# Five edits in a two-layer decoder kernel: units of a scan among its first prelude, a quantisation loop as a pipeline, a delta rule's copies, four-head attention by portions, ternary weights beside the last norm

## The reference

```python
# 1 selective scan: causal 4-tap convolution, low-rank delta, then over time, 16 states per channel
h = dA * h + dBu;  y = einsum('bdn,bn->bd', h, c)
# 2 smooth-quantised expert, for each of the 4 batches: w1 (512 x 512), w2 (512 x 256)
s = maximum(sqrt(maximum(amax_x, EPS) / maximum(amax_w, EPS)), EPS)
xs = x / s;  ws = w * s
x_q = clip(round(xs / x_scale), -127, 127);  w_q = clip(round(ws / w_scale), -127, 127)
out = x_q @ w_q.T * x_scale * w_scale.T          # twice, with silu(gate) * up between
# 3 a mixture of 8 experts and a shared one
# 4 delta rule, 16 heads of 128, 512 steps of time
S = S * exp(g);  vd = (v - S @ k) * beta;  S = S + outer(k, vd);  o = S @ q
o = o * rsqrt(mean(o * o) + EPS) * o_norm_w * sigmoid(gate);  out = o @ Wo
# 5 cross attention, 32 heads of 16, with rotary positions
w = softmax(q k^T / 4);  attn = w @ v
# 6 ternary feed-forward, hidden width 1408
wq = clip(round(w / mean(|w|)), -1, 1);  xq = round(x * 127 / max|x|)
h = silu(bitlinear(x, w1)) * bitlinear(x, w2);  bitlinear(h, w3)
```

## Time and profile before

| what | us |
| --- | --- |
| median of three runs (6689.74 to 6696.33) | 6691.91 |
| profiled run | 6693.45 |
| its span | 6691.8 |
| PE busy | 5326.8 (80%) |
| PEld busy | 3517.8 (53%) |
| DVE busy | 4030.0 (60%) |
| ACT busy | 2628.2 (39%) |
| POOL busy | 2044.4 (31%) |

### The profile page before, as it was taken

One profiled execution on the slowest core, in us unless ns is written; L12 is line 12 of the kernel. 1 busy time (PEld: TensorE's weight loads), 2 busy tenths in 40 slices (PEclk: granted clock), 3 DMA queues, 4 the chain that ended last, 5 costly groups with the idle time before them and its releaser, 6 DMA issues. The chain is left out here.

```text
span 6691.8 us, 83945 instructions
## 1 busy us (share of the span) xinstructions
PE 5326.8 (80%) x24965; PEld 3517.8 (53%) x24965; DVE 4030.0 (60%) x6738; ACT 2628.2 (39%) x4831; POOL 2044.4 (31%) x2589
## 2 busy tenths in 40 slices
PE   4889437999478888888888888888887669999946
PEld 2666324555245556555565555655555335555513
DVE  4777663222277666666666666666666246666566
ACT  4555211111144444444444444444443116666512
POOL 2556100201244434344343443434434050000100
PEclk8999758999689999999999999999998789999978
DMA  2011004344311111111111111111110021111010
GB/s 55 27 26 26 19 19 180 117 135 149 109 48 46 31 48 41 37 46 37 48 41 37 46 37 48 41 37 36 37 48 19 23 85 49 43 43 43 30 52 25
DMA packets 349792, 344.90 MB, mean 52 GB/s; under 512 B 99552, under 2 KB 252640, under 8 KB 348160
## 3 DMA queue, kind: packets, MB, share of 16 engines
q1 hardware_dynamic: 335472, 286.73, 14.6%
q0 software_dynamic: 13984, 54.01, 2.3%
HBM read 264.76 MB, written 75.89 MB: 51 GB/s over the span
## 5 line engine op out<-in xcount | busy, mean ns | idle before, releaser
L1706 POOL TENSOR_TENSOR delta_rule_suffix<-delta_rule_suffix,delta_rule_prefix 128x256 f32<-128x256 f32 x448 | 498.9, 1114 | 1268.7 <-ACT delta_rule_prefix L1800 743.5
L2520 PE MATMUL attend_out_ps<-attend_probsT,attend_v_head 128*128 128x512 f32 x1024 | 481.5, 593 | 0.0
L2070 PE MATMUL delta_rule_level<-delta_rule_qk_second,delta_rule_k_first 128*128 128x128 f32 x3072 | 427.8, 283 | 51.8 <-DVE delta_rule_L_small L1879 40.3
L2046 PE MATMUL delta_rule_proj<-delta_rule_hT,delta_rule_w_qkv 128*128 128x512 f32 x1024 | 466.5, 599 | 0.0
L1697 POOL TENSOR_TENSOR delta_rule_k_first<-delta_rule_qk,delta_rule_suffix 128x256 f32<-128x256 f32 x384 | 303.3, 790 | 512.6 <-PE delta_rule_level L2058 485.5
L2070 PEld LDWEIGHTS delta_rule_level<-delta_rule_qk_second,delta_rule_k_first 128*128 128x128 f32 x3072 | 385.8, 195 | 103.2 <-issue 81.8
L2547 DVE TENSOR_REDUCE attend_top<-attend_scores 128x1 f32<-128x512 f32 x512 | 328.5, 683 | 158.3 <-PE attend_scores L2502 158.3
L1947 DVE TENSOR_TENSOR delta_rule_prefix<-delta_rule_prefix 128x256 f32<-128x256 f32 x448 | 287.5, 642 | 226.0 <-PE delta_rule_level L2058 187.3
L472 DVE TENSOR_TENSOR_SCAN scan_hs<-scan_decay,scan_inp 128x512 f32<-128x512 f32 x256 | 307.9, 1216 | 189.2 <-PE scan_inp L534 91.0
L309 POOL TENSOR_TENSOR scan_hc<-scan_hs,scan_c_rows 128x512 f32<-128x512 f32 x256 | 333.1, 1308 | 272.2 <-DVE scan_hs L472 253.4
L1890 DVE TENSOR_TENSOR delta_rule_qk_second<-delta_rule_qk,delta_rule_prefix 128x512 f32<-128x512 f32 x448 | 337.9, 754 | 45.9 <-issue 10.3
(11 more groups left out here) (463 smaller groups left out, 12036.1 us busy)
## 6 DMA issues: line engine op xcount, KB each, us to landing
moe_w_d<-in_w_down SPq DMA_DIRECT2D x39, 512.0 KB, 4.4
scan_c_rows<-bc_dram SPq DMA_DIRECT2D x64, 256.0 KB, 3.8
delta_rule_w_qkv<-in_kda_wq SPq DMA_DIRECT2D x64, 256.0 KB
delta_rule_w_qkv<-in_kda_wk SPq DMA_DIRECT2D x64, 256.0 KB
delta_rule_w_qkv<-in_kda_wv SPq DMA_DIRECT2D x64, 256.0 KB
delta_rule_inv_beta<-beta_dram SPq DMA_DIRECT2D x64, 256.0 KB
delta_rule_w_o<-in_kda_wo SPq DMA_DIRECT2D x64, 256.0 KB, 5.0
small_dram<-delta_rule_L_small SPq DMA_DIRECT2D x64, 256.0 KB, 2.0
```

What stands on the lines that cost most here:

```text
L1706: pool.tensor_tensor(first, first, whole_second, ALU.mult).then_inc(suffix_done, 1)
L2046: last = pe.matmul(to, w_qkv[p][:, i, k, :], hT[:, b % 2, k, :], start=(k == 0), stop=(k == DT - 1))
L2070: last = pe.matmul(level_ps[(i + 1) % 2][:, c, :], left, qk_second[:, i % 2, :, c * CHUNK // 2:(c + 1) * CHUNK // 2], start=True, stop=True)
L2520: last = pe.matmul(out_ps[:], v_head[:, j, i, :], probsT[:, j % 2, i, :], start=(j == 0 and i == 0), stop=(j == H - 1 and i == TPB - 1))
```

## The change

Five parts, one for each of five blocks.

**Scan.** Unit 0 goes at slot 36 of the first prelude, and 28 units of batch 0 share its remaining slots. The other 36 units of batch 0 take the 64 chores of batch 1 between them. The diagonals of batch 0 are made in slots 24 to 39.

```diff
+        FIRST_UNIT_AT = 36
             for j in range(UNITS):
                 chores(0, j)
-            for b in range(B):
+                if j >= FIRST_UNIT_AT:
+                    unit(0, j - FIRST_UNIT_AT)
+            for i in range(FIRST_UNIT_AT):
+                unit(0, UNITS - FIRST_UNIT_AT + i)
+                for j in range(i * UNITS // FIRST_UNIT_AT, (i + 1) * UNITS // FIRST_UNIT_AT):
+                    chores(1, j)
+            for b in range(1, B):
```

```diff
+    JOBS = [(b, lin) for lin in range(2) for b in range(B)]
+            def pipeline(*stages):
+                for at in range(N + len(stages) - 1):
+                    for slot in range(SLOTS):
+                        for d in reversed(range(len(stages))):
+                            if 0 <= at - d < N:
+                                stages[d](slot, at - d)
...
+                    def quantize(slot, i):
+                        if second:
+                            act.wait_ge(inv_ready, m + 1)
+                            reach(act, quantized, m - 1)
+                            for r in range(HALF_ROWS):
+                                last = act.activation(rounded[:, m % 2, r, 0:width], rows_ps[m % 2][r][:, 0:width], ACT.Identity,
+                                                      bias=round_up[:, 0:1], scale=row_inv[:, m % 2, r:r + 1])
+                            last.then_inc(rounded_done, 1)
+                            if q > 0:
+                                copy_turned(i, q - 1)
```

```diff
-        SQUARE_SLOT, NORM_SLOT, LN_SLOT, EXP_SLOT, GATED_SLOT, OUT_SLOT, ADD_SLOT = 12, 13, 14, 14, 17, 23, 25
+        SQUARE_SLOT, NORM_SLOT, LN_SLOT, EXP_SLOT, GATED_SLOT, OUT_SLOT, ADD_SLOT = 12, 13, 20, 20, 26, 23, 26
+        VD_COPY_SLOTS = (1, 4, 6, 10)
-                    if slot < 3 * CHUNKS and slot % 3 == 1:
-                        c = slot // 3
+                    if slot in VD_COPY_SLOTS:
+                        c = VD_COPY_SLOTS.index(slot)
                 def tail(slot, n):
+                    project(slot, n)
                     back(slot, n)
-                    project(slot, n)
-                            pe.wait_ge(o_inv_done, n + 1)
+                            pe.wait_ge(o_ln, n + 1)
```

```diff
+    GROUP = 4
+    WEIGH_AT = 1
+    COLS = 2 * X_DIM
-                    last = pe.matmul(out_ps[:], v_head[:, j, i, :], probsT[:, j % 2, i, :],
-                                     start=(j == 0 and i == 0), stop=(j == H - 1 and i == TPB - 1))
+                    for q in range(GROUP):
+                        j = half * GROUP + q
+                        last = pe.matmul(out_ps[q * COLS:(q + 1) * COLS, :], v_head[:, j, i, :], probsT[:, j, i, :],
+                                         start=(half == 0 and i == 0), stop=(half == 1 and i == TPB - 1))
...
                         turn(n, j, i)
-                        if i % 2 == 1 and not first:
-                            weigh(*before, i - 1)
-                            weigh(*before, i)
+                        if i == WEIGH_AT:
+                            if j >= GROUP:
+                                weigh(n, 0, j - GROUP)
+                            elif not first_tile:
+                                weigh(n - 1, 1, j)
```

```diff
+                        act.activation(flat_weights(i), w[:, i, :], ACT.Abs, accum_out=part[:, i:i + 1]).then_inc(part_done, 1)
+                        if i > 0:
+                            act.wait_ge(inv_ready, i)
+                            act.activation(w[:, i - 1, :], w[:, i - 1, :], ACT.Identity, bias=round_up[:, 0:1],
+                                           scale=inv[:, i - 1:i]).then_inc(rounded_up, 1)
...
+                        dve.tensor_scalar(w[:, i, :], w[:, i, :], ROUND, -1.0, ALU.subtract, ALU.max)
+                        dve.tensor_scalar(flat_weights(i), w[:, i, :], 1.0, None, ALU.min)
...
                         for c, (lo, n) in enumerate(FFN_CHUNKS):
+                            if c == 1 and not first:
+                                turn_act(t - 1)
```

More of the change, by code:

```diff
@@ new lines, in _, with scales, output @@
+                    for j in range(2):
+                        sp.wait_ge(w_loaded[j], 16 * N // 2)
+                @block.gpsimd
+                def _(pool):
+                    pool.memset(round_up[:], ROUND).then_inc(round_made, 1)
+                    def scales(slot, i):
+                        pass
+                    def output(slot, i):
+                        if slot == 0:
+                            along = row_scale[:, i % 2, JOBS[i][1], :]
+                            pool.wait_ge(inv_ready, PARTS_OF_JOB * (i + 1))
+                            reach(pool, acc_done, acc_item(i - 2, 0) + 1 if i >= 2 else 0)
+                            for r in range(TPB):
+                                last = pool.tensor_scalar(spread[:, i % 2, r, :], g["ones"][:], along[:, r:r + 1], None, ALU.mult)
+                            last.then_inc(spread_done, 1)
+                    pipeline(scales, scales, output)
@@ L708, in _ @@
-                            if lin == 0:
-                                dve.drain()
-                                dve.wait_ge(silu_done, b + 1)
-                                dve.tensor_tensor(actT[:], silu[:], up[:], ALU.mult)
+                            reach(dve, rounded_done, m - 1)
+                            dve.reciprocal(row_inv[:, m % 2, :], scale).then_inc(inv_ready, 1)
+                        else:
+                            dve.wait_ge(rounded_done, m + 1)
+                            reach(dve, q_turned, m - 1)
+                            dve.tensor_scalar(q_rows[:, m % 2, :, 0:width], rounded[:, m % 2, :, 0:width],
+                                              ROUND, None, ALU.subtract).then_inc(quantized, 1)
@@ L713, in _ @@
+                    pipeline(stats, quantize, output)
                 @block.scalar
                 def _(act):
[L715 to L734 removed]
@@ new lines, in output @@
+                    def output(slot, i):
+                        b, lin = JOBS[i]
+                        p = i % 2
+                        if slot == 1:
+                            copy_turned(i, PARTS_OF_JOB - 1)
+                            item = acc_item(i, 0)
+                            act.wait_ge(acc_done, item + 1)
+                            reach(act, job_out, i - 1)
+                            act.activation(scale_row[:, p, :], acc[item % 2][:], ACT.Copy).then_inc(acc_read[item % 2], 1)
+                            act.wait_ge(acc_read[item % 2], item // 2 + 1)
+                            act.nop().then_inc(scale_row_copied, 1)
+                        elif slot == SILU_SLOT and lin == 0:
+                            item = acc_item(i, KT[1])
+                            for j in (item - 1, item):
+                                act.wait_ge(acc_read[j % 2], j // 2 + 1)
+                            act.activation(silu[:, p], gate[:, p], ACT.Silu).then_inc(silu_done, 1)
@@ L783 @@
+                    pipeline(scales, quantize, output)
 EXPERTS, TOP_K, HIDDEN = 8, 2, 352
@@ L2896, in step @@
                         for c, (lo, n) in enumerate(FFN_CHUNKS):
+                            if c == 1 and not first:
+                                copy_act(t - 1)
                             j = buffer(p, c)
```

485 lines of the change are left out of this document (281 added, 204 removed).

## The result

The changed kernel takes 6414.49 us (median, 6410.6 to 6422.86), the kernel before 6694.11 in the same comparison: a ratio of 0.9585, 95% interval 0.9568 to 0.9601. The forecast was 6449, with a range of 6345 to 6612. The profiled run took 6422.86 us, the longest of the four, with a span of 6421.3.

A forecast was written before the change was run, and what follows sets the result against it. Each stage has its own bound: TensorE in attend, waits in the delta rule, engines taking turns in the quantised layer. Savings of 10, 80, 67, 25, 30 and 32 us sum to 244: 6693.45 - 244 = 6449, range 6345 to 6612.

The forecast's parts named there:

- scan: Scan stage: units among the first prelude save 10 us; bounds 29 saved and 14 lost.
- ternary layer: Ternary layer: turning and copying activations behind the first chunk saves 2.3 us a step, 32 in all (20 to 38).
- first-kind job: Quantised layer: one of four pipeline jobs of the first kind among eight, about 29 us each.
- the handovers: Quantised layer: DVE and ACT hand over inside each part, so DVE's floor of 135 us is not reached; 222 instead.
- Term (b): Delta rule: Ln and Exp with their table loads leave slot 14, so R's copy comes earlier: 1.5 us gained per unit.
- Term (a): Delta rule: the state copy on ACT moves from slot 7 to 6: 0.3 us lost per unit, at best 1.5 gained.
- the rival at 0.27: Attend: all four portions run at once, saving 96 us instead of 25, for 6378 us in all; chance 0.27.
- The staircase step: Attend: portions overlap only partly, weighing 2.15 us, step 5.87, 25 us saved; the likeliest case, chance 0.44.
- the queue's floor: Attend: the queue needs 5.3 us to issue a head's six loads, so a head can't be shorter.
- the packing: Scan: 36 units taking all 64 chores cost 8 us extra for being packed more densely.
- The bound of 14 us lost: Scan: worst case, ACT's diagonals of the next batch fall into the last 8 units, 14 us lost.
- DVE's own sum: Ternary layer: DVE's work alone bounds the new step, at 9.7 us.

The follow-up runs named there:

- Experiment 10: The changed kernel with the quantised layer's rounding on DVE again (two passes from PSUM, then the subtraction): 6419.32 us.
- Experiment 1: The changed kernel with DVE's three taps of the convolution of v in delta rule slots 9, 9, 10 instead of 7, 7, 9: 6261.12 us.
- experiment 5: The changed kernel with the four matmuls of an attend weighing step all in one portion of the accumulator: 6661.35 us.
- Experiment 7: The changed kernel with DVE's product of the first chunk ahead of the next tile's quantisation in the ternary layer: 6397.88 us.
- first combined kernel: The changed kernel with first-batch diagonals one by one, no unit in the first prelude, v taps at 9, 9, 10, k loads on GpSimd, first chunk before quantisation: 6147.93 us.
- second combined kernel: The first combined kernel with DVE's scaling of k moved from slot 6 to slot 8 of the delta rule: 6100.52 us.
- experiment 2: The changed kernel with the third copy of vd back at slot 7 instead of 6 in the delta rule: 6410.3 us.

## Why the prediction was right, and where it was not

**The sum.** Forecast 244 us saved, measured 280 by the medians and 270.5 by the profiled runs. That it came so near is in part luck: its likeliest case for attend was wrong and 42 us too low, and two other terms (scan, ternary layer) were too high by 31 us together.

**Quantised layer: right.** 86 us for 80. A first-kind job took 29.4 us between two maxima of x (forecast 29), a second-kind job 22.3 (25). Experiment 10 shows that DVE's sum doesn't bind: 31 us more of DVE cost 7. That the handovers do is argued from DVE's and ACT's waits for each other; experiment 10 took two of them out as it added the work, so their price was not measured alone.

**Delta rule: right sum, one term undervalued.** The forecast unit of 51.2 us is the measured one. Term (b), 1.5 us, measured 1.1 (from the kernel before) or 1.7 us (with the copy at slot 6). Term (a), 0.3 lost, measured 0.5 lost alone and nothing beside (b). So the parts of one stage don't add, although its total came out. What I named as late next, the state update behind the taps, is where the wait went (37.7 to 259.4 us); but I took it for a small loss, gave 1.5 us as the most that the taps could be worth, and didn't say that it was the largest gain left. Experiment 1 put it at 2.6 us a unit. The copy's move makes TensorE wait longer in both kernels, by 0.8 us a unit before and 1.0 beside (b) (averages over 59 units). In the first it gets 0.3 of that back in shorter busy time, in the second 0.9: this is the share of the lower clock, 20% against 14% of the time in the second. The sum had no term for the clock. Why the lower clock takes the larger share with the copy at slot 7 stays open; no run held the clock fixed.

**Attend: the rival at 0.27 came true.** The staircase step failed: that a portion's two passes follow each other while the next portion starts only behind the first. Measured is w = 1.00, near the lower bound of 0.86; experiment 5 shows that different portions run at once and the same one doesn't (3.56). With w = 1.0 the queue's floor decides, as the rival said, at 5.36 us a head. It gave 96 us, from 5.3 us for every head; the queue took 5.44 on average, which leaves 0.61 x 128 = 78. Measured were 67 to 79, the difference among runs being in what follows the last load. Of the Trainium skill, "TensorE: Matmul & The Clock Gate", section Measured speedup vs the span model, has 2.38x for three column tiles. By that the weighing would be 3.44 / 2.38 = 1.45 us, an estimate, and not the "about 1.2" of the prediction; the queue's floor would decide with either. Here four gave 3.6x, in line with "TensorEngine Tiling (Array Packing)", section Theoretical Speedup, "Up to 4×". Of the drain at a change of tiling mode (the same page, section Key Properties) the trace shows nothing of size: turns follow the portions 1.00 us after their start.

**Scan: wrong sign.** The start was right to 0.1 us. The term that failed is the packing: I gave 8 us to 64 chores among 36 units, and it was 18 (129.1 us where 111 were counted without it). The slots 36 to 63 took 63 us instead of 57.5. The bound of 14 us lost contained it. The forecast counted work per engine; the idle 44.5 us before 36 scans end mostly with ACT's decay and TensorE's input (22.4 and 13.4). That each unit stood behind two chores there is read from the order of the program; no run changed it alone.

**Ternary weights: right.** 31 for 30. ACT's passes took 4.9 to 5.1 us each (estimate 5.5), but began 11.3 us after the stage instead of 9.4. The first load had landed after 10.0; ACT first waits for the norm's variance:

```profile
6180.82 0.21 ACT L2851 ACTIVATE ternary_rstd<-ternary_rstd 128x16 f32<-128x16 f32 x1 [9.88 <-DVE ternary_rstd L2895]
6180.94 4.88 ACT L2855 ACTIVATE ffn_w1q<-ternary_w 128x5632 bf16<-128x5632 f32 x1
```

**Ternary layer: too high.** "What is left is DVE's own sum" was wrong: the ring of two hidden buffers ties the third chunk to DVE's read of the first. DVE's order is the same in the kernel before; the forecast didn't look at it. Experiment 7 changes it, and the step is 9.5, near the 9.7 of the forecast.

## What to carry to other kernels

When a wait is taken away, look up at once what stands in front of the next user on its own engine: here three taps that were not urgent cost 2.6 us a unit, more than the move that was made. Here narrow matmuls gained only side by side in different portions, and once they did, the six small DMAs of a step were the bound. Work packed densely beside other work cost more than its sum in the scan; moving only the piece that stood in front (the diagonals) won 8 us where moving whole units lost 7.5. Look at TensorE's busy time beside its waits: here 57 us less of the one was 57 us more of the other.

## What the runs showed of the hardware

**Four 32-column portions.** Eight float32 instructions into four different portions took 1.00 us, eight into one portion 3.56. Four instructions of 32 columns one after another in the scan's prelude took 1.88 us, as four of 128 columns in attend.

**The clock after a wait.** TensorE's wait of 4.33 us in the delta rule is followed by a stretch at the lower of its two clocks. The granted clock (third column from the end) before the wait's end, just behind it, some five microseconds later, and after that:

```profile
2976.00:2978.00 2.00, 0.00 (x0) 0.00 (x0) 1.44 (x2) 1.48 (x5) 0.70 (x1) 1.00 0.03 3
2979.00:2980.00 1.00, 0.62 (x3) 0.50 (x2) 0.79 (x2) 0.00 (x0) 0.00 (x0) 0.50 0.46 174
2984.00:2985.00 1.00, 1.00 (x6) 1.00 (x6) 0.77 (x2) 0.00 (x0) 0.86 (x1) 0.50 0.38 143
2986.00:2988.00 2.00, 2.00 (x11) 1.23 (x10) 1.77 (x3) 0.07 (x1) 1.49 (x3) 1.00 0.00 0
```

0.50 is 1.2 GHz, 1.00 is 2.4 GHz. The stretch held work. In the unit before, a level product of eight instructions took 1.91 us in it and one of the same shape 1.06 after it. So the time after such a wait is worth less; that the wait is what brings the stretch is not shown:

```profile
2932.59 1.91 PE L2174 MATMUL delta_rule_level<-delta_rule_qk_second,delta_rule_qk 128*128 128x128 f32 x8
...
2936.54 1.06 PE L2174 MATMUL delta_rule_level<-delta_rule_qk_second,delta_rule_k_first 128*128 128x128 f32 x8
```
But the clock doesn't simply follow the waits. It was 0.93 in the changed kernel, 0.95 in the first combined kernel and 0.96 in the second, each with less waiting; yet experiment 2 has less waiting than the changed kernel, no wait over 2.91 us in 40 steady units, and a clock of 0.90. A stretch at the lower clock comes about once a unit in all of them, also in the second combined kernel, where no wait in 40 steady units is over 2.1 us. It holds 6.9 us a unit in the changed kernel, 10.1 in experiment 2, 4.9 in experiment 1 and 3.5 in the second combined kernel. What sets it is open.

**Issuing DMAs.** SyncE issued six in 5.36 us, 0.89 each; GpSimd three in 1.83, 0.61 each. The three are loads of k alone, the six of q and k.
